# The relation layer of a graph network on one core: row fetching split into four pieces with the one-hot block stationary, and a new order of the work around it

## The chip, the cores and the metric

The kernel runs on one core of one Trainium2 chip. The metric is the device time of one execution in microseconds (us). A core has a matrix engine (TensorE, PE in the profile, with PEld for its weight loads), a vector engine (VectorE, DVE), a scalar engine (ScalarE, ACT), GpSimd (POOL) and a queue engine (SyncE, SP). The engines run their own instruction lists and wait for each other on semaphores. PE adds its products up in eight PSUM banks of 128 partitions by 512 fp32 values.

## The reference, cut to what matters

Two graph layers stand one behind the other. The first (two SAGE layers, a norm and a layer norm) is made with a dense adjacency and is not touched. The second, the relation layer, is what the change is about: 62,500 edges used of 6,250 nodes with 128 features, 32 relation types built from 8 basis matrices.

```python
hsrc = h[src]                       # rows of the edges' source nodes
coef = w_comp[etype]                # [edges, 8]
for b in range(8):
    msg = msg + hsrc @ weight[b] * coef[:, b][:, None]
msg = msg * norm
node_repr = jax.ops.segment_sum(msg, dst, num_segments=6250)
node_repr = jax.nn.relu(node_repr + bias)
x = layernorm(x + node_repr)
```

The edges are ordered by destination node.

## The kernel before

The first layer is built and run until about 2075 us of the profiled execution; from there to about 3830 us runs the relation layer. It works in STEPS = 114 steps. A step takes 10 tiles of 128 edges in order of destination (STEP_TILES), whose source rows GpSimd gathers from DRAM by an indirect DMA each (L797), and, in the first GROUPS = 112 steps, a group of PER = 4 further tiles of 128 edges that were sorted by their source node. The source nodes of a group lie in one of 7 classes of 7 blocks of 128 nodes (CLASS_BLOCKS), so their rows need no DMA: PE fetches them out of node rows that stay in SBUF, with a one-hot matrix. The node rows are kept as three bf16 parts whose sum is the fp32 value (XS part 0, XS part 1, and LOW).

What each engine does in step s:

* DVE makes `matrix` (L1719 to L1728: the place of an edge's node in a window times norm times the 8 coefficients), `wide_matrix` for the sorted group (L1735, L1736, L1741), the one-hot `ST2` of group s+2 (`sources`, L1749, 7 instructions of 512 columns), and adds PE's sums of every tile into rings of sums over nodes in SBUF (`tile_added`, L1769, 10 instructions, and `wide_added`, L1778, 4 instructions). Before the tile sums it reads the positions in the ring from a table (L1753 and the register loads with it, which the profile does not count as busy).
* PE makes `tiles_summed` (L1310: 5 fp32 products of 64 columns, twice per step), `sources` for the group of step s+2 (L1284: 21 bf16 products of 512 columns into bank 2, in the pieces 9, 6 and 6), `wide_summed` (L1327: 4 fp32 products of 336 columns), `coefficients` for step s+2 (L1266, L1270), `sources_turned` (L1319: 4 fp32 transposes of the fetched rows of group s+1), and in the 46 steps in which blocks of nodes are complete `block_multiplied` (L1346: 8 basis products for each of 51 blocks). 13 results are transposed at L1357.
* ACT makes `relations` (L972 to L981: the one-hot of edge types for step s+3), copies coefficients out of PSUM (L989), copies the fetched rows (L995) and the transposed rows (L1002), and takes a multiplied block with the bias (`block_taken`, L1021) and clears its place in the ring (L1026).
* SP issues the loads of edge types (L624, L629) and source rows (L637) and stores the results (L644).

Every engine works through its list in the order written. What comes out of PE goes through a ring of six PSUM banks (UNIT_BANKS); a unit (tile half, wide tile, turned group or result) waits in `unit_bank_free` until the unit six places before it has been added up by DVE, copied by ACT or taken. Blocks wait on DVE's additions (s_addg, s_adds) and on the coefficients copied (s_coefc); DVE's next additions into the ring wait for nothing else than their own bank except where ACT has cleared a block.

Of the kernel before, what the change touches and what calls it, by code (L numbers as in the profile page):

```python
# [91 lines left out]
SOURCE_PARTS = [(0, 3), (3, 5), (5, CLASS_BLOCKS)]  # L92
# [74 lines left out]
for step in range(STEPS):  # L167
    if step == 0:
        UNITS.append((0, "turn", 0))
# [4 lines left out]
    if step + 1 < GROUPS:  # L174
        UNITS.append((step + 1, "turn", 0))
# [60 lines left out]
def regular(nc, flag, x, src, dst, etype, w, w1, lin1, b1, lin2, b2, Wrel, wcomp, brel, out):  # L236
    with ExitStack() as ctx:
# [97 lines left out]
        GT = [unused[:, j * 512:(j + 1) * 512] for j in range(2)]  # L335
# [122 lines left out]
        s_turned = sem("sources_turned_copied")  # L458
# [342 lines left out]
        def _(act):  # L801
# [189 lines left out]
            def sources_copied(i):  # L991
                act.wait_ge(s_gs, i + 1)
                if i >= 2:
                    act.wait_ge(s_u, UNIT[i - 2, "turn", 0] + 1)
                nc.scalar.activation(GT[i % 2], bank(2), ACT.Copy).then_inc(s_gc, 1)  # L995

            def turned_copied(i):
                n = UNIT[i, "turn", 0]
                act.wait_ge(s_u, n + 1)
                if i >= 2:  # L1000
                    act.wait_ge(s_u, UNIT[i - 2, "wide", PER - 1] + 1)
                nc.scalar.activation(G2[i % 2].rearrange("p t c -> p (t c)"), bank(UNIT_BANKS[n % RING_BANKS]), ACT.Copy).then_inc(s_turned, 1)  # L1002
# [38 lines left out]
            turned_copied(0)  # L1041
            relations(2)
            sources_copied(1)
            for s in range(OUT_AT[-1] + 3):
                if KEPT_CHUNK + s < len(CHUNKS):
                    halved(KEPT_CHUNK + s)
                for n in events_in(s - 1):
                    block_taken(n)
# [5 lines left out]
                if s + 2 < STEPS:  # L1054
                    coefficients_copied(s + 2)
                if s + 1 < GROUPS:
                    turned_copied(s + 1)
                if s + 3 < STEPS:
                    relations(s + 3)

        @block.tensor
        def _(pe):
# [195 lines left out]
            def coefficients(s):  # L1258
# [3 lines left out]
                before = events_to(s - 3, lambda n: True)  # L1262
# [11 lines left out]
            def sources(i, part):  # L1274
                if part == 0:
# [3 lines left out]
                first = group_of(i) // ROUNDS_SORTED * CLASS_BLOCKS  # L1279
# [6 lines left out]
                if end == CLASS_BLOCKS:  # L1286
                    last.then_inc(s_gs, 1)

            def unit_bank_free(n):

                if n >= RING_BANKS:
# [5 lines left out]
                    elif kind == "turn":  # L1297
# [1737 lines left out]
```

## Time and profile before

| | us |
|---|---|
| median of three executions | 3764.12 |
| their range | 3760.8 to 3773.42 |
| the profiled execution: its span and own time | 3868.7 |
| first layer in it, about | 0 to 2075 |
| relation layer in it, about | 2075 to 3830 |

The profiled execution is 104.6 us (2.8%) longer than the median of the three, so times read from its trace are of a somewhat slower execution. In a row of a timeline stand the start, the duration, engine, line, operation, tiles and the count, and in brackets how long the engine was idle ahead of it and which instruction released it. "issue" means that nothing in the profile shows a wait; "remote" is a wait whose releaser the profile does not find. Ends of PE instructions are modelled, so the distance of two starts tells the pace better than a duration.

### The profile page before, as it was taken

What the parts mean: (1) busy time and instruction counts of PE and PEld (TensorE: products, weight loads), DVE (VectorE), ACT (ScalarE), POOL (GpSimd) and SP (SyncE); (2) the same over time, 40 slices, a digit from 0 to 9 for tenths busy, and PEclk for the clock granted to TensorE, in tenths of its full rate; (3) what the DMA queues carried; (4) which work ended last, traced back from release to release, by engine and by line L of the source; (5) the groups of instructions that cost most, each with busy time, mean ns of one, the idle gap of its engine ahead of it and who ended that gap; (6) DMA issues with size and microseconds to landing.
All of it is one profiled execution on the core that took longest, in us unless ns stands there. A gap on an engine that the chain in (4) does not pass through costs nothing.

```text
span 3868.7 us, 52705 instructions
## 1 busy us (share of the span) xinstructions
PE 3418.3 (88%) x17077; PEld 2281.2 (59%) x17077; DVE 2465.0 (64%) x4684; ACT 1351.6 (35%) x3452; POOL 2415.7 (62%) x2636
## 2 busy tenths in 40 slices
PE   3999999998999999999996888888988888988885
PEld 3899999984533344544443555556655556655554
DVE  7999999995776663022033666666656666666664
ACT  5999999990000000010002222222222222222221
POOL 5888888880036775555523666666666666666663
PEclk6999999999999999999998889888888888888897
DMA  6677777778779999999993222232222222222222
GB/s 185 192 206 205 206 208 208 208 205 291 263 233 256 269 259 269 301 271 275 293 298 93 65 66 70 60 78 70 70 57 71 65 74 67 73 65 69 67 66 46
DMA packets 532789, 618.45 MB, mean 160 GB/s; under 512 B 74011, under 2 KB 460127, under 8 KB 532399
## 3 DMA queue, kind: packets, MB, share of 16 engines
q1 hardware_dynamic: 478895, 528.52, 46.9%
q0 software_dynamic: 53616, 86.51, 8.9%
q8 instruction: 140, 2.29, 0.2%
q14 instruction: 138, 1.13, 0.1%
HBM read 445.83 MB, written 168.99 MB: 159 GB/s over the span
## 4 chain that ended last, share of the span: by engine, by line
PE 49%; ACT 19%; DVE 8%; issue 8%; DMA 7%; another core or an unknown queue 7%; DVEq 2%; POOL 1%; SPq 0%; ACTq 0%; POOLq 0%
PE PS L1231 21%; ACT arena L845 11%; PE PS L1284 10%; DMA arena<-adjacency 7%; ACT arena L861 6%; PE PS L1310 5%; PE PS L1327 5%; PE PS L1270 2%; PE PS L1119 2%; PE PS L1346 1%; DVE XT L1769 1%; PE PS L1319 1%; DVEq L1753 1%; DVE H L1749 1%
## 5 line engine op out<-in xcount | busy, mean ns | idle before, releaser
L797 POOL DMA_INDIRECT arena<-x_table,rec x1140 | 1159.6, 1017 | 613.0 <-issue 309.8
L776 POOL DMA_INDIRECT sorted_records<-arena x428 | 505.9, 1182 | 556.2 <-PE PS L1231 476.5
L1119 PE MATMUL PS<-arena 128*98 128x128 f32 x6272 | 761.6, 279 | 46.3 <-DVE arena L1508 13.0
L1119 PEld LDWEIGHTS PS<-arena 128*98 128x98 f32 x6272 | 708.4, 166 | 95.9 <-issue 50.4
L733 POOL TENSOR_SCALAR arena<-iota,H,arena 128x98 f32<-128x98 f32 x980 | 674.2, 702 | 91.7 <-PE PS L1119 89.2
L1284 PE MATMUL PS<-H,X 128*128 128x512 bf16 x1568 | 548.9, 436 | 74.5 <-issue 66.9
L845 ACT ACTIVATE arena<-arena 128x98 f32<-128x98 f32 x1568 | 582.9, 686 | 12.7 <-DVE arena L1506 12.6
L1231 PE MATMUL PS<-arena,X 128*128 128x512 f32 (+1 forms) x1274 | 541.4, 577 | 39.3 <-DMA arena<-adjacency 38.6
L1231 PE MATMUL PS<-arena,H 128*128 128x512 f32 (+1 forms) x1274 | 527.8, 570 | 16.0 <-DMA arena<-adjacency 15.5
L861 ACT ACTIVATE arena<-PS 98x1024 f32<-98x1024 f32 x392 | 519.6, 1325 | 12.5 <-PE PS L1119 12.5
L1769 DVE TENSOR_TENSOR XT<-XT,PS 128x64 f32 x1140 | 252.1, 221 | 421.6 <-issue 188.8
L1508 DVE TENSOR_TENSOR arena<-PS,H 128x2048 f32<-128x2048 f32 x196 | 447.0, 2280 | 0.0
L1687 DVE TENSOR_TENSOR arena<-arena 128x1536 f32<-128x1536 f32 (+1 forms) x192 | 343.9, 1791 | 157.2 <-DMA arena<-adjacency 151.5
L1231 PEld LDWEIGHTS PS<-arena,X 128*128 128x128 f32 x1274 | 237.4, 192 | 322.4 <-issue 193.3
L1231 PEld LDWEIGHTS PS<-arena,H 128*128 128x128 f32 x1274 | 238.5, 190 | 293.8 <-issue 215.3
L1310 PEld LDWEIGHTS PS<-arena 128*128 128x128 f32 x2280 | 320.6, 213 | 78.9 <-issue 46.8
L1310 PE MATMUL PS<-arena 128*128 128x64 f32 x2280 | 323.3, 292 | 46.5 <-issue 33.4
L1327 PE MATMUL PS<-arena 128*128 128x336 f32 x896 | 313.5, 472 | 43.5 <-issue 35.5
L1284 PE MATMUL PS<-H,arena 128*128 128x512 bf16 x784 | 337.6, 431 | 1.2 <-issue 1.0
L1778 DVE TENSOR_TENSOR arena<-arena,PS 128x336 f32 x448 | 224.7, 501 | 173.9 <-remote 75.7
L1284 PEld LDWEIGHTS PS<-H,X 128*128 128x128 bf16 x1568 | 172.5, 117 | 257.4 <-issue 162.9
L995 ACT ACTIVATE rec<-PS 128x512 f32<-128x512 f32 x112 | 66.7, 596 | 682.7 <-remote 439.7
(259 smaller groups left out, 3139.6 us busy)
## 6 DMA issues: line engine op xcount, KB each, us to landing
arena<-adjacency SPq DMA_DIRECT2D x294, 768.0 KB
adjacency<-arena SPq DMA_DIRECT2D x196, 784.0 KB
arena<-adjacency SPq DMA_DIRECT2D x98, 832.0 KB
arena<-x_table,rec POOLq DMA_INDIRECT x1140
XT<-sorted_source_rows SPq DMA_DIRECT2D x112, 128.0 KB
arena<-in_edge_type SPq DMA_DIRECT2D x226, 48.0 KB
arena<-in_edge_type SPq DMA_DIRECT2D x226, 32.0 KB
XT<-sorted_relations SPq DMA_DIRECT2D x448, 8.0 KB
```

The source lines that it names most:

```text
L733: last = nc.gpsimd.tensor_scalar(S1[:, r, :], iota[:, 0:M1], K1T[:, v:v + 1], WWT[:, v:v + 1], ALU.is_equal, ALU.mult)
L776: pool.indirect_dma_start(rec2_d, bass.IndirectOffsetOnAxis(ap=SLOT[:, t:t + 1], axis=0), R4[:, t, :], None).then_inc(s_scat, 16)
L797: pool.indirect_dma_start(G[:, n % HELD_UNITS * UNIT_TILES + i, :], None, x1_d, bass.IndirectOffsetOnAxis(ap=SRC[:, t:t + 1], axis=0)).the ...
L845: nc.scalar.activation(S1[:, r, :], S1[:, r, :], ACT.Copy, scale=WWT[:, v:v + 1]).then_inc(s_wa, 1)
L861: nc.scalar.activation(ST[0:M1, n % 3, q * GROUP * P:(q + 1) * GROUP * P], PS[0:M1, q * GROUP * P:(q + 1) * GROUP * P], ACT.Copy).then_inc ...
L1119: last = nc.tensor.matmul(bank(2 * q + j // 4, P, j % 4 * P)[0:M1, :], S1[:, r, :], S2[:, r, :], start=True, stop=True)
L1231: last = nc.tensor.matmul(bank(bank0 + c, nb * P), (X, H1)[l][:, k, :], AB[n % 4][:, off:off + nb * P], start=(k == 0), stop=(k == NBLK - 1))
L1284: last = nc.tensor.matmul(bank(2), rows_part, ST2[i % 2][:, j, :], start=(j == 0 and a == 0), stop=(j == CLASS_BLOCKS - 1 and a == 2))
L1310: last = nc.tensor.matmul(bank(UNIT_BANKS[n % RING_BANKS], BASIS, j * BASIS), G[:, half % HELD_UNITS * UNIT_TILES + j, :], C[s % 2][:, fir ...
L1327: nc.tensor.matmul(bank(UNIT_BANKS[n % RING_BANKS], WIDE_BASIS), G2[i % 2][:, c, :], C2[i % 2][:, c, :, :].rearrange("p b j -> p (b j)"), ...
L1508: nc.vector.tensor_tensor(S2[:, whole, :], bank(4, P).unsqueeze(1).to_broadcast([P, BATCH, P]), each(K2T, n).to_broadcast([P, BATCH, P]), ...
L1687: nc.vector.tensor_tensor(ACC[p % 2][:, 0:width], ACC[p % 2][:, 0:width], AB[n % 4][:, 0:width], ALU.add).then_inc(s_acc, 1)
```

## The change

`sources(i, c)` makes the fetched rows of one tile c of 128 edges at a time. The one-hot piece `ST2[:, j, c*128:(c+1)*128]` is the stationary side, the 128 columns of a part of the node rows are the moving side, and the result is [edge, feature], as `wide_summed` needs it. 84 products of 128 columns take the place of 21 of 512 columns. `sources_turned` on PE, `turned_copied` on ACT, the tile GT, the semaphore sources_turned_copied and the unit "turn" in the ring are gone. The four pieces stand in four places of PE's step. `coefficients(s+2)` moves ahead of the blocks; a block waits for the coefficients of step+4 rather than step+3. On ACT `relations(s+3)` and `coefficients_copied(s+2)` move from the end of a step to its start.

```diff
-SOURCE_PARTS = [(0, 3), (3, 5), (5, CLASS_BLOCKS)]
...
             def sources_copied(i):
                 act.wait_ge(s_gs, i + 1)
                 if i >= 2:
-                    act.wait_ge(s_u, UNIT[i - 2, "turn", 0] + 1)
-                nc.scalar.activation(GT[i % 2], bank(2), ACT.Copy).then_inc(s_gc, 1)
-
-            def turned_copied(i):
-                n = UNIT[i, "turn", 0]
-                act.wait_ge(s_u, n + 1)
-                if i >= 2:
                     act.wait_ge(s_u, UNIT[i - 2, "wide", PER - 1] + 1)
-                nc.scalar.activation(G2[i % 2].rearrange("p t c -> p (t c)"), bank(UNIT_BANKS[n % RING_BANKS]), ACT.Copy).then_inc(s_turned, 1)
+                nc.scalar.activation(G2[i % 2].rearrange("p t c -> p (t c)"), bank(2), ACT.Copy).then_inc(s_gc, 1)
...
             for s in range(OUT_AT[-1] + 3):
                 if KEPT_CHUNK + s < len(CHUNKS):
                     halved(KEPT_CHUNK + s)
+                if s + 3 < STEPS:
+                    relations(s + 3)
+                if s + 2 < STEPS:
+                    coefficients_copied(s + 2)
                 for n in events_in(s - 1):
                     block_taken(n)
...
                 if s + 2 < GROUPS:
                     sources_copied(s + 2)
-                if s + 2 < STEPS:
-                    coefficients_copied(s + 2)
-                if s + 1 < GROUPS:
-                    turned_copied(s + 1)
-                if s + 3 < STEPS:
-                    relations(s + 3)
...
-                before = events_to(s - 3, lambda n: True)
+                before = events_to(s - 4, lambda n: True)
...
-            def sources(i, part):
-                if part == 0:
+            def sources(i, c):
+                first = group_of(i) // ROUNDS_SORTED * CLASS_BLOCKS
+                if c == 0:
                     pe.wait_ge(s_st2, i + 1)
                     if i:
                         pe.wait_ge(s_gc, i)
-                begin, end = SOURCE_PARTS[part]
-                pe.wait_ge(s_low, CHUNK_OF[first + end - 1] + 1)
-                for j in range(begin, end):
+                for j in range(CLASS_BLOCKS):
+                    if c == 0 and i < CLASSES:
+                        pe.wait_ge(s_low, CHUNK_OF[first + j] + 1)
                     for a, rows_part in enumerate((XS[:, first + j, 0, :], XS[:, first + j, 1, :], LOW[:, first + j, :])):
-                        last = nc.tensor.matmul(bank(2), rows_part, ST2[i % 2][:, j, :],
+                        last = nc.tensor.matmul(bank(2, D, c * D), ST2[i % 2][:, j, c * P:(c + 1) * P], rows_part,
                                                 start=(j == 0 and a == 0), stop=(j == CLASS_BLOCKS - 1 and a == 2))
...
-                pe.wait_ge(s_turned, i + 1)
+                pe.wait_ge(s_gc, i + 1)
...
-                pe.wait_ge(s_coefc, min(step + 3, STEPS))
+                pe.wait_ge(s_coefc, min(step + 4, STEPS))
...
             for s in range(OUT_AT[-1] + 1):
+                ahead = s + 2 < GROUPS
                 if s < STEPS:
                     tiles_summed(s, 0)
-                if s + 2 < GROUPS:
+                if ahead:
                     sources(s + 2, 0)
                 if s < GROUPS:
                     wide_summed(s, 0)
                     wide_summed(s, 1)
-                if s + 2 < GROUPS:
+                if ahead:
                     sources(s + 2, 1)
+                if s + 2 < STEPS:
+                    coefficients(s + 2)
                 for n in events_in(s - 1):
                     block_multiplied(n)
                 if s < GROUPS:
                     wide_summed(s, 2)
                     wide_summed(s, 3)
+                if ahead:
+                    sources(s + 2, 2)
                 if s < STEPS:
                     tiles_summed(s, 1)
-                if s + 2 < GROUPS:
-                    sources(s + 2, 2)
-                if s + 2 < STEPS:
-                    coefficients(s + 2)
-                if s + 1 < GROUPS:
-                    sources_turned(s + 1)
+                if ahead:
+                    sources(s + 2, 3)
```

PE's list before, from the end of the second row-fetching piece of a step in which a block is multiplied, to its first transposes (H is part of the kept one-hots and rows, wcd the relation coefficients, Wr the basis matrices):

```order
L1284 MATMUL PS<-H,arena 128x512
L1346 MATMUL PS<-XT,Wr 128x128 [waits messages_rectified,coefficients_copied,gathered_sums_added]
L1346 MATMUL PS<-XT,Wr 128x128 x7
L1327 MATMUL PS<-arena 128x336 [waits wide_matrix_made,sources_turned_copied,sorted_sums_added]
L1327 MATMUL PS<-arena 128x336 [waits wide_matrix_made,sources_turned_copied,gathered_sums_added]
L1310 MATMUL PS<-arena 128x64 [waits nodes_gathered3,matrix_made,sources_turned_copied]
...
L1266 MATMUL PS<-wcd,XT 128x32 [waits messages_rectified,coefficients_copied,relations_marked]
L1270 MATMUL PS<-wcd,arena 128x32 x2
L1270 MATMUL PS<-wcd,arena 128x16
L1319 MATMUL PS<-ident,rec 128x128 [waits sources_copied,gathered_sums_added]
```

PE's list after the change at the same block, from the end of the second piece:

```order
L1267 MATMUL PS<-X,H 128x128 x2
L1267 MATMUL PS<-arena,H 128x128
L1249 MATMUL PS<-wcd,XT 128x32 [waits messages_rectified,coefficients_copied,relations_marked]
L1253 MATMUL PS<-wcd,arena 128x32 x2
L1253 MATMUL PS<-wcd,arena 128x16
L1319 MATMUL PS<-XT,Wr 128x128 [waits messages_rectified,coefficients_copied,gathered_sums_added]
L1319 MATMUL PS<-XT,Wr 128x128 x7
L1300 MATMUL PS<-arena 128x336 [waits wide_matrix_made,sources_copied,sorted_sums_added] x2
```

The coefficients' products now stand directly ahead of the block, whose wait on coefficients_copied is for these same coefficients, and the wide tiles behind the block wait on sources_copied alone.

ACT's list before, of the same step, from the block it takes to the last instruction of `relations`:

```order
L1021 ACTIVATE H<-PS,bcol 128x128 [waits basis_sums_made,blocks_multiplied]
L1026 ACTIVATE XT<-zero 128x8x128
L995 ACTIVATE rec<-PS 128x512 [waits basis_sums_made,sources_multiplied]
L989 ACTIVATE XT<-PS 128x112 [waits wide_matrix_made,matrix_made,coefficients_multiplied]
L1002 ACTIVATE arena<-PS 128x512 [waits basis_sums_made]
L972 ACTIVATE H<-arena,rel_of 128x256 [waits types_spread1,coefficients_multiplied]
L973 ACTIVATE H<-arena,rel_of 64x128
L976 ACTIVATE XT<-XT,rel_of 128x128 [waits sorted_types_spread1]
L978 ACTIVATE H<-H,ones 128x256 [waits relations_apart]
L979 ACTIVATE H<-H,ones 64x128
L981 ACTIVATE XT<-XT,ones 128x128
```

ACT's list after the change, of the same step:

```order
L965 ACTIVATE H<-arena,rel_of 128x256 [waits types_spread1,coefficients_multiplied]
L966 ACTIVATE H<-arena,rel_of 64x128
L969 ACTIVATE XT<-XT,rel_of 128x128 [waits sorted_types_spread1]
L971 ACTIVATE H<-H,ones 128x256 [waits relations_apart]
L972 ACTIVATE H<-H,ones 64x128
L974 ACTIVATE XT<-XT,ones 128x128
L982 ACTIVATE XT<-PS 128x112 [waits wide_matrix_made,matrix_made,coefficients_multiplied]
L1007 ACTIVATE H<-PS,bcol 128x128 [waits basis_sums_made,blocks_multiplied]
L1012 ACTIVATE XT<-zero 128x8x128
L988 ACTIVATE arena<-PS 128x512 [waits basis_sums_made,sources_multiplied]
```

`relations`, with its waits on the loaded edge types, and the copy of the coefficients now stand ahead of the block and its clearing. The lists of DVE, GpSimd and SyncE are the same before and after.

## Rows read from the trace of the kernel before

**Rows 1.** The page: busy time of each engine.

```profile
PE 3418.3 (88%) x17077; PEld 2281.2 (59%) x17077; DVE 2465.0 (64%) x4684; ACT 1351.6 (35%) x3452; POOL 2415.7 (62%) x2636
```

**Rows 2.** Windows, 2165 to 3830 us: length, busy PE, PEld, DVE, ACT, POOL, clock.

```profile
2165.00:3830.00 1665.00, 1425.71 (x7330) 974.64 (x7330) 1063.34 (x3167) 430.34 (x1066) 1100.37 (x1084) 0.87 0.27 68
```

**Rows 3.** Timeline of PE, one step at full clock.

```profile
3027.17 1.23 PE L1310 MATMUL PS<-arena 128*128 128x64 f32 x10
3028.23 0.59 PE L1284 MATMUL PS<-H,X 128*128 128x512 bf16 x2
...
3033.73 1.22 PE L1310 MATMUL PS<-arena 128*128 128x64 f32 x10
3034.79 0.59 PE L1284 MATMUL PS<-H,X 128*128 128x512 bf16 x2
...
3036.09 0.30 PE L1266 MATMUL PS<-wcd,XT 128*128 128x32 f32 x2
...
3037.09 0.66 PE L1319 MATMUL PS<-ident,rec 128*128 128x128 f32 x4
3037.58 0.56 PE L1310 MATMUL PS<-arena 128*128 128x64 f32 x2
```

**Rows 4.** Timeline of DVE, one step without long waits.

```profile
3354.44 1.63 DVE L1769 TENSOR_TENSOR XT<-XT,PS 128x64 f32 x5 [2.79 <-issue]
...
3362.65 0.50 DVE L1778 TENSOR_TENSOR arena<-arena,PS 128x336 f32 x1
...
3367.63 0.93 DVE L1769 TENSOR_TENSOR XT<-XT,PS 128x64 f32 x3 [2.22 <-issue]
```

**Rows 5.** Groups by line, 2165 to 3830 us: count, busy, mean ns, idle before.

```profile
L797 POOL DMA_INDIRECT arena<-x_table,rec x1084 | 1101.8, 1016 | 564.4 <-issue 294.2 <-PE PS L1310 124.9 <-remote 118.0
```

**Rows 6.** Waits of DVE, 2165 to 3830 us: total, times, longest.

```profile
DVE arena L1778 <- remote: 75.7, 29, 6.7
...
DVE XT L1769 <- remote: 45.1, 14, 4.9
...
DVE arena L1778 <- ACT arena L1026: 18.1, 7, 4.9
DVE arena L1778 <- PE PS L1310: 11.1, 10, 4.7
DVE arena L1778 <- PE PS L1327: 9.1, 7, 4.7
DVE arena L1778 <- ACT XT L1026: 6.9, 5, 2.0
```

**Rows 7.** Timeline of PE, early: pairs of a load and a 1-column product.

```profile
1002.84 1.96 PE L1184 MATMUL PS<-ones_h,H 128*128 128x1 bf16 x28
```

**Rows 8.** Timeline of PE at half clock.

```profile
2959.42 1.06 PE L1284 MATMUL PS<-H,X 128*128 128x512 bf16 x2
2960.28 0.63 PE L1284 MATMUL PS<-H,arena 128*128 128x512 bf16 x1
```

**Rows 9.** Groups of the whole span: the transposes.

```profile
L1319 PE MATMUL PS<-ident,rec 128*128 128x128 f32 x448 | 84.7, 316 | 6.8 <-issue 6.8
```

**Rows 10.** Timeline of SyncE behind a stored result.

```profile
2789.63 0.41 SPq L644 DMA_DIRECT2D out<-H  x1
...
2792.55 1.84 SPq L629 DMA_DIRECT2D arena<-in_edge_type  x4
```

**Rows 11.** Timeline of ACT there: `relations`, first and last instruction.

```profile
2787.94 0.50 ACT L972 ACTIVATE H<-arena,rel_of 128x256 f32<-128x256 int32 x1
...
2789.76 0.38 ACT L981 ACTIVATE XT<-XT,ones 128x128 f32<-128x128 f32 x1
```

**Rows 12.** Timelines of PE and ACT: a block multiplied, a ring place cleared.

```profile
2965.67 1.95 PE L1346 MATMUL PS<-XT,Wr 128*128 128x128 f32 x16
...
2972.79 1.04 ACT L1026 ACTIVATE XT<-zero 128x1024 f32<-128x1024 f32 x1
```

**Rows 13.** Timeline of DVE there: the third wide tile.

```profile
2803.94 0.50 DVE L1778 TENSOR_TENSOR arena<-arena,PS 128x336 f32 x1
```

More of the change, by code:

```diff
@@ L167 @@
 for step in range(STEPS):
-    if step == 0:
-        UNITS.append((0, "turn", 0))
     UNITS.append((step, "tile", 0))
@@ L173 @@
     UNITS.append((step, "tile", 1))
-    if step + 1 < GROUPS:
-        UNITS.append((step + 1, "turn", 0))
     UNITS += [(step, "result", m) for m in range(len(OUT_AT)) if OUT_AT[m] == step]
@@ L334, in regular @@
         ST2 = [h1_flat[:, j * HALF_ST2:(j + 1) * HALF_ST2].bitcast(BF16).rearrange("p (k e) -> p k e", e=PER * P) for j in range(2)]
-        GT = [unused[:, j * 512:(j + 1) * 512] for j in range(2)]
         G2 = [cut(17280 + j * PER * D, PER * D).rearrange("p (t c) -> p t c", c=D) for j in range(2)]
@@ L457, in regular @@
         s_u = sem("basis_sums_made")
-        s_turned = sem("sources_turned_copied")
         s_bp = sem("blocks_multiplied")
@@ L1040, in _ @@
             sources_copied(0)
-            turned_copied(0)
             relations(2)
@@ L1278, in sources @@
                         pe.wait_ge(s_gc, i)
-                first = group_of(i) // ROUNDS_SORTED * CLASS_BLOCKS
-                begin, end = SOURCE_PARTS[part]
-                pe.wait_ge(s_low, CHUNK_OF[first + end - 1] + 1)
-                for j in range(begin, end):
+                for j in range(CLASS_BLOCKS):
+                    if c == 0 and i < CLASSES:
+                        pe.wait_ge(s_low, CHUNK_OF[first + j] + 1)
                     for a, rows_part in enumerate((XS[:, first + j, 0, :], XS[:, first + j, 1, :], LOW[:, first + j, :])):
-                        last = nc.tensor.matmul(bank(2), rows_part, ST2[i % 2][:, j, :],
+                        last = nc.tensor.matmul(bank(2, D, c * D), ST2[i % 2][:, j, c * P:(c + 1) * P], rows_part,
                                                 start=(j == 0 and a == 0), stop=(j == CLASS_BLOCKS - 1 and a == 2))
-                if end == CLASS_BLOCKS:
+                if c == PER - 1:
                     last.then_inc(s_gs, 1)
@@ L1296, in unit_bank_free @@
                         pe.wait_ge(s_adds, added_wide(step, i))
-                    elif kind == "turn":
-                        pe.wait_ge(s_turned, step + 1)
                     else:
@@ L1312, in tiles_summed @@
                 last.then_inc(s_u, 1)
-            def sources_turned(i):
-                n = UNIT[i, "turn", 0]
-                unit_bank_free(n)
-                pe.wait_ge(s_gc, i + 1)
-                for c in range(PER):
-                    last = nc.tensor.transpose(bank(UNIT_BANKS[n % RING_BANKS], P, c * P), GT[i % 2][:, c * P:(c + 1) * P], ident[:])
-                last.then_inc(s_u, 1)
             def wide_summed(i, c):
@@ L1364, in _ @@
             for i in range(2):
-                for part in range(len(SOURCE_PARTS)):
-                    sources(i, part)
-                if i == 0:
-                    sources_turned(0)
+                for c in range(PER):
+                    sources(i, c)
             pe.wait_ge(s_zero, 2)
             for s in range(OUT_AT[-1] + 1):
+                ahead = s + 2 < GROUPS
                 if s < STEPS:
                     tiles_summed(s, 0)
-                if s + 2 < GROUPS:
+                if ahead:
                     sources(s + 2, 0)
```

## The prediction

> **What bounds the kernel now.** I read the busy shares first. PE is busy 88% of the span, DVE 64% [rows 1], and in the relation layer PE has 1425.7 of 1665 us [rows 2]. That looks like a PE bound, and a change that adds 63 products to each step would then be paid in full. A share doesn't tell why an engine is busy, though: PE's clock is 0.87 in this window [rows 2], so part of its work ran at half speed, and a PE that is late only because it has time does no harm. So I read single steps next. At full clock a PE step runs from 3027.17 to 3037.58, 10.41 us, from its first tile products to those of the next step [rows 3]. A DVE step without long waits runs from 3354.44 to 3367.63, 13.19 us, from one step's first ring addition to the next's, with table reads in it that the profile shows as "issue" [rows 4]. GpSimd's gathers take (1101.8 + 294.2) / 1084 = 1.29 us each, "issue" included, 12.9 us for ten [rows 5]. DVE, with GpSimd close behind it, is the longest of the three by 2.8 us over PE.
>
> Does that account for the layer? The window holds 109 steps (1084 gathers of ten a step, and a few), 15.3 us each. 109 steps of 13.19 us are 1438 us. Waits of DVE without a known releaser add 75.7 + 45.1 = 120.8 us in 43 cases, and waits with PE or ACT as releaser 18.1 + 11.1 + 9.1 + 6.9 = 45.2 us in 29 cases [rows 6]. That makes 1604 of 1665 us; about ten results of some 5 us on DVE (an estimate: they are in no row here) fill most of the rest. So at most some 45 us of the layer is visibly owed to a late PE or ACT. The 120.8 us are close to the 104.6 us by which the profiled execution is longer than the median, and I take them to be its own: the sum below is made on the median of 3764, and the same differences would hold on the 3868.7 us of the profiled execution.
>
> **The change part by part.**
>
> *Row fetching.* Now 21 products of 512 columns; six of them stand between 3034.79 and 3036.09, 0.217 us each [rows 3], 4.55 us a step. Then 84 products of 128 columns, each with a weight load of its own. No row shows that pair, so I bound it. From below: a quarter of 0.217, 0.054 us, if the load hides wholly behind the product ahead of it. From above: 28 pairs of a bf16 load and a product of only one column took 1.96 us, 0.070 us each [rows 7], which is the pace of loads alone; if load and product hid nothing of each other it would be 0.070 + 0.054 = 0.124. The profile calls PEld overlapping with PE and 974.6 us of loads lie beside 1425.7 us of products in 1665 us [rows 2], so they overlap; the time is then the larger of the two, 0.054 to 0.070. I take 0.060, as some of the 28 ends are pipeline latency: 84 × 0.060 = 5.04 us, +0.5 us a step. At half clock two products of 512 columns took 2960.28 − 2959.42 = 0.86 us, 0.43 each [rows 8], so a quarter is 0.107: 84 of them take 9.0 us, as 21 took, and the load is hidden sooner.
>
> The Trainium skill speaks against the change here: "TensorE: Matmul & The Clock Gate", section "Back-to-back issue gap", gives a sustained stream of load and product pairs of 128 columns about 81 ns each, against 56 ns for an isolated gap. By that estimate the pieces would take 6.8 us. The trace has no stream of such pairs; its nearest row gives 0.070.
>
> *Transposes.* 448 are gone: four took 3037.58 − 3037.09 = 0.49 us [rows 3], 84.7 us busy and 6.8 us idle over the span [rows 9]. Together with the pieces PE's step is 10.41 + 0.50 − 0.49 = 10.4 us, unchanged, still 2.8 us under DVE's: no cost and no gain. ACT's copy of 0.6 us a step goes too; ACT is busy 430 of 1665 us [rows 2], so it is worth nothing by itself.
>
> *Way of a late PE to the next wide tile.* Where PE is late behind a block, its catching up counts. Before, from the wide tiles behind a block to those of the next step: tiles 1.06 (3033.73 to 3034.79), row fetching 1.30, coefficients 1.00 (3036.09 to 3037.09), transposes 0.49, tiles 1.06, row fetching 9 × 0.217 = 1.95; 6.86 us [rows 3]. After: 3 × 21 × 0.060 + 2 × 1.06 = 5.90. That is 0.96 us less. The 29 waits [rows 6] are the places where it can count: at most 29 × 0.96 = 28 us, at least nothing. About half of them (12, on ACT's clearing of a block) end at a block in the same step, which the shorter way does not bring forward, and at the others a part is swallowed by waits behind them: I take half, −14 us.
>
> *Coefficients ahead of the block.* In 46 steps the block now stands behind 1.00 us of coefficient products and a wait for ACT's copy of them, some 0.65 us (an estimate: PE's drain, and a copy of a fifth of the 512-column copy). The third wide tile comes 1.65 us later in PE's step. DVE asks for it 3362.65 − 3354.44 = 8.21 us after its step's first addition [rows 4], in which it does its matrices and the one-hot, so I cost it at nothing; without that cover it would be 46 × 1.65 = 76 us at most.
>
> *ACT's new order.* `relations` waits for edge types from SyncE; behind it now stand the coefficients' copy, the block, its clearing and the copy of fetched rows, and behind these PE's block and DVE. SyncE is late where a result is stored: the store stood at 2789.63 and the last type load began at 2792.55 + 1.84 = 2794.39 [rows 10]. With some 2 us to land (0 to 5.5 as bounds; no row shows one of these landings), `relations` of 2.2 us (2787.94 to 2790.14 [rows 11]), 0.3 us for the copy, 1.95 us for a block [rows 12], an estimated 0.4 us for taking it and 1.04 us for clearing [rows 12], that is 2802.3; DVE took the third wide tile at 2803.94 [rows 13]. The margin is 1.6 us, −1.8 at the late bound and 3.7 at the early one. Six steps are of this kind (a stored result and a block in one step); with a late bound and a second block of 2 to 3 us the loss is 6 × 4.7 = 28 us; I take 8.
>
> Sum: 3764 + 0 − 14 + 8 = 3758 us.
>
> **The rivals.**
>
> *PE is the real bound (gain).* For it: 88% busy and 1425.7 of 1665 us [rows 1, 2]. Then the 91.5 us of transposes [rows 9] come back less what the pieces cost, 112 × 0.5 = 56, so −35 at 0.060 and −72 at 0.056: between 3729 and 3692, say 3710. Against it: only 45.2 us of DVE's waits name PE or ACT. Chance 0.20.
>
> *Nothing moves.* Late steps come from DVE's and GpSimd's own work, the credit and the loss are both taken up by the waits that follow: 3764 ± 5. Chance 0.12.
>
> *ACT's order costs (slower).* The place is `relations` at the head of a step with a stored result; from a landing later than 3.6 us behind the issue it decides. Price 28 us, and no credit: 3792. For it: SyncE's issues alone take 4.8 us there [rows 10]. Against it: the margin worked out above. Chance 0.15.
>
> *The loads don't hide (slower).* The point from which it decides is the pace at which PE's mean step reaches DVE's 13.19. PE's is 10.41 − 0.49 − 4.55 = 5.37, and blocks add 51 × 1.95 / 112 = 0.89, the wait ahead of them 0.27; so 6.53 + 84 × t reaches 13.19 at t = 0.079. At 0.124 PE's step is 16.9 us against a mean of (1665 − 120.8) / 109 = 14.2: +2.7 × 112 = +302, 4066 us. Just above 0.079, with a half clock here and there, 10 to 40 us: about 3790. Chance 0.13, nearly all of it for the small price. The page named above puts the pace, 81 ns, at this very point.
>
> **How the numbers follow.** The forecast has the rest, 0.40, with a range of its own of 3738 to 3772. Of the time of this kernel 0.3% is 11.3 us, about what its measurement can tell from no change: 3753 to 3775. The forecast of 3758 lies just inside; of its 0.40 I give 0.17 to faster, 0.22 to the same, 0.01 to slower. Faster: 0.17 + 0.20 = 0.37. The same: 0.22 + 0.12 + 0.02 of the slower rivals = 0.36. Slower: 0.01 + 0.26 = 0.27. The range reaches into the gain (3700) and takes in both small prices (3800); beyond stand the end of the gain and a pace far over 0.079, under 2 in 10 together.
>
> **What the profile of the changed kernel would show.** The pace of the 128-column products, from starts: 0.054 to 0.070 proves the first step, 0.08 and more the last rival. DVE's steps without waits stay at 13.2 us, and its waits on PE and ACT fall from 45 us to about 31 if the credit is right; they rise at the wide tiles, with ACT's clearing or PE's block as releaser, in the six steps with a stored result if ACT's order costs, and `relations` is then seen to wait for a DMA. PE's step at full clock stays near 10.4 us, with a gap of about 0.65 us ahead of a block. PE's clock may change with the 84 short products in place of the long ones; the median would show it only if PE became the last to end. The prediction is wrong if DVE's step is not what paces the layer, or if waits that I gave to the profiled execution are in every execution and follow from PE's list of instructions, which grows by half.

## The result, and the profile after

On the chip on which the kernel before took 3764.03 us (median of six), the changed kernel took 3785.76 us (median of six, 3779.66 to 3789.87). The medians are 21.7 us apart; the ratio with its 95% interval, 1.0048 (1.0033 to 1.0063), makes it 18 us (12 to 24). The forecast was 3758 us, by a small gain.

A second result came with the experiments. On three other chips the same two programs took 3880 and 4759, 3894 and 4755, and 3868 and 4738 us: ratios 1.2244, 1.2225 and 1.2256. On a fourth the kernel before took 3744 us. So there are two kinds of chip for this kernel; I call them first kind (3744 to 3764 us before) and second kind (3868 to 3911 us before). One chip of the second kind came twice, with 3894 and 3911 us, and no chip was seen to change its kind. The profile of before [rows 1 to 13] with its 3868.7 us looks like the second kind, and its median came from the first. Not only its time says so. PE's waits ahead of row fetching without a releaser, 2165 to 3830 us, in before and then in before_again, which ran on a second-kind chip:

```profile
PE PS L1284 <- issue: 55.6, 26, 7.0
PE PS L1284 <- issue: 73.8, 39, 8.2
```

No profile of a first-kind chip, or of a kernel with direct loads (below), has more than 1.5 us of them.

The page and the windows of the changed kernel, profiled on the chip of the 3786 us (columns as in [rows 2]):

```profile
PE 3328.4 (88%) x23685; PEld 2497.3 (66%) x23685; DVE 2467.1 (65%) x4684; ACT 1294.2 (34%) x3340; POOL 2413.3 (64%) x2636
...
2165.00:3750.00 1585.00, 1353.74 (x13915) 1203.96 (x13914) 1090.68 (x3238) 381.43 (x973) 1149.80 (x1111) 0.92 0.30 73
```

6608 more products, and PE is still 88% busy. The clock is 0.92 in place of 0.87, but on a chip of the other kind; before_plain below, without the change, has 0.92 too. PE's waits, and those of DVE, in 2165 to 3740 us (total, times, longest):

```profile
PE PS L1267 <- DVE H L1721: 86.1, 55, 2.5
PE PS L1319 <- issue: 56.9, 35, 8.6
PE PS L1300 <- DVE arena L1713: 49.0, 61, 1.9
```

```profile
DVE XT L1741 <- PE PS L1300: 116.5, 45, 3.2
...
DVE XT L1741 <- PE PS L1291: 13.1, 8, 2.8
DVE arena L1750 <- ACT XT L1012: 4.7, 3, 2.4
DVE arena L1750 <- PE PS L1300: 4.3, 11, 1.0
...
DVE arena L1750 <- ACT arena L1012: 3.5, 1, 3.5
DVE arena L1750 <- PE PS L1291: 2.9, 10, 0.6
```

PE waits for DVE's one-hot and for the wide matrix, which is how a PE looks that has time. The 116.5 us in the first row of DVE stand ahead of the tile sums, where DVE reads its table: 2.6 us each, where the same place without a releaser takes 2.4 (151.6 us in 64 cases), so hardly more than that reading. The "remote" waits, 120.8 us in [rows 6], are gone: they belong to the other kind of chip, for before_again has 63.1 and 43.0 us of them in the same window. New are PE's waits of up to 8.6 us ahead of a block (L1319), and on ACT the wait of `relations` for edge types, which stands at 131 us in the groups by line:

```profile
L965 ACT ACTIVATE H<-arena,rel_of 128x256 f32<-128x256 int32 x55 | 27.5, 500 | 40.6 <-DMA arena<-in_edge_type 40.6
...
L965 ACT ACTIVATE arena<-arena,rel_of 128x256 f32<-128x256 int32 x54 | 27.0, 501 | 90.5 <-DMA arena<-in_edge_type 90.5
```

Most of it costs nothing, since ACT is ahead. Where it costs, one sees in a step with a stored result and a block. The timelines of SyncE, ACT, PE and DVE in step 52:

```profile
2878.09 0.41 SPq L637 DMA_DIRECT2D out<-H  x1
...
2881.00 1.86 SPq L622 DMA_DIRECT2D arena<-in_edge_type  x4
```

```profile
2885.37 0.51 ACT L965 ACTIVATE H<-arena,rel_of 128x256 f32<-128x256 int32 x1 [13.24 <-DMA arena<-in_edge_type]
...
2887.49 0.24 ACT L982 ACTIVATE XT<-PS 128x112 f32<-128x112 f32 x1
2891.44 0.37 ACT L1007 ACTIVATE H<-PS,bcol 128x128 f32<-128x128 f32 x1 [3.71 <-PE PS L1319]
2891.70 1.05 ACT L1012 ACTIVATE XT<-zero 128x1024 f32<-128x1024 f32 x1
```

```profile
2887.83 3.57 PE L1319 MATMUL PS<-XT,Wr 128*128 128x128 f32 x16 [7.80 <-issue]
2891.24 1.30 PE L1300 MATMUL PS<-arena 128*128 128x336 f32 x4
```

```profile
2883.34 1.64 DVE L1741 TENSOR_TENSOR XT<-XT,PS 128x64 f32 x5 [2.21 <-issue]
...
2892.89 0.50 DVE L1750 TENSOR_TENSOR arena<-arena,PS 128x336 f32 x1 [1.39 <-ACT XT L1012]
...
2894.96 1.64 DVE L1741 TENSOR_TENSOR XT<-XT,PS 128x64 f32 x5 [0.85 <-PE PS L1291]
```

The loads are issued until 2882.86, `relations` starts at 2885.37, 2.5 us later, the coefficients are copied at 2887.73, and only then may PE start its block, though these coefficients were multiplied 8 us before and the block's sums were ready as well. The block then takes 3.57 us where it took 1.95 [rows 12]: after 7.8 us without work PE runs its first products at half clock. The windows of the changed kernel around it (columns as in [rows 2], the clock third from the end):

```profile
2884.00:2887.80 3.80, 0.00 (x0) 0.00 (x0) 3.20 (x11) 2.33 (x7) 0.69 (x1) 0.53 0.52 116
2887.80:2891.20 3.40, 3.37 (x16) 3.40 (x17) 3.33 (x9) 0.00 (x0) 0.00 (x0) 0.52 0.11 31
2891.20:2893.00 1.80, 1.80 (x18) 1.34 (x18) 0.41 (x2) 1.31 (x2) 0.00 (x0) 1.00 0.25 62
```

The granted clock is at the lower of the two levels, 1.2 GHz, for nearly all of the block, and at 2.4 GHz behind it. DVE's third wide tile waits 1.39 us for ACT's clearing, and 0.85 us more are lost at the next tile sums. The step takes 16.1 us. The 1.6 us by which the block is longer are more than either of these waits: at full clock this step would have lost next to nothing (an estimate from these rows, not run).

### The profile page after: what moved, and what is told of

It reads as the page before. It is cut to its first block, busy times and chain, and to the rows that moved or that the text cites. A ratio compares the mean times of both kernels' runs of the same rounds, so it can differ in the third digit from the quotient of the medians.

```text
span 3785.2 us, 65588 instructions
## 1 busy us (share of the span) xinstructions
PE 3328.4 (88%) x23685; PEld 2497.3 (66%) x23685; DVE 2467.1 (65%) x4684; ACT 1294.2 (34%) x3340; POOL 2413.3 (64%) x2636
## 4 chain that ended last, share of the span: by engine, by line
PE 35%; DVE 21%; ACT 18%; DMA 10%; issue 9%; DVEq 6%; POOL 1%; SPq 0%; POOLq 0%
PE PS L1214 20%; ACT arena L838 11%; DMA arena<-adjacency 10%; ACT arena L854 6%; DVE H L1721 5%; DVE XT L1741 5%; DVEq L1725 5%; PE PS L1267 4%; PE PS L1300 3%; DVE arena L1750 2%; PE PS L1319 2%; PE PS L1291 2%; PE PS L1102 2%; DVE arena L1700 1%; DVEq L1741 1%
## 5 line engine op out<-in xcount | busy, mean ns | idle before, releaser
L790 POOL DMA_INDIRECT arena<-x_table,rec x1140 | 1179.4, 1035 | 463.8 <-issue 325.2
L769 POOL DMA_INDIRECT sorted_records<-arena x428 | 483.8, 1130 | 626.3 <-PE PS L1214 548.3
L1267 PE MATMUL PS<-X,H 128*128 128x128 bf16 x6272 | 610.5, 227 | 89.2 <-DVE H L1721 86.1
L1267 PEld LDWEIGHTS PS<-X,H 128*128 128x128 bf16 x6272 | 521.6, 103 | 163.2 <-DVE H L1721 96.0
L1267 PE MATMUL PS<-arena,H 128*128 128x128 bf16 x3136 | 583.2, 227 | 0.0
L1300 PE MATMUL PS<-arena 128*128 128x336 f32 x896 | 337.7, 503 | 49.1 <-DVE arena L1713 49.0
L1291 PE MATMUL PS<-arena 128*128 128x64 f32 x2280 | 299.2, 280 | 27.3 <-DVE H L1778 19.8
L1267 PEld LDWEIGHTS PS<-arena,H 128*128 128x128 bf16 x3136 | 319.6, 102 | 0.0
L1291 PEld LDWEIGHTS PS<-arena 128*128 128x128 f32 x2280 | 280.5, 196 | 30.6 <-DVE H L1778 21.4
L1478 DVE TENSOR_TENSOR arena<-PS,H 128x1078 f32<-128x1078 f32 x196 | 250.6, 1278 | 41.2 <-PE PS L1102 34.1
```

The source lines that it names most:

```text
L769: pool.indirect_dma_start(rec2_d, bass.IndirectOffsetOnAxis(ap=SLOT[:, t:t + 1], axis=0), R4[:, t, :], None).then_inc(s_scat, 16)
L790: pool.indirect_dma_start(G[:, n % HELD_UNITS * UNIT_TILES + i, :], None, x1_d, bass.IndirectOffsetOnAxis(ap=SRC[:, t:t + 1], axis=0)).the ...
L1267: last = nc.tensor.matmul(bank(2, D, c * D), ST2[i % 2][:, j, c * P:(c + 1) * P], rows_part, start=(j == 0 and a == 0), stop=(j == CLASS_B ...
L1291: last = nc.tensor.matmul(bank(UNIT_BANKS[n % RING_BANKS], BASIS, j * BASIS), G[:, half % HELD_UNITS * UNIT_TILES + j, :], C[s % 2][:, fir ...
L1300: nc.tensor.matmul(bank(UNIT_BANKS[n % RING_BANKS], WIDE_BASIS), G2[i % 2][:, c, :], C2[i % 2][:, c, :, :].rearrange("p b j -> p (b j)"), ...
```

## The experiments

All kernels of one group ran on one chip; "beside" stands the median of the kernel before on that chip, and the ratio behind a time is to it. The loads on GpSimd were replaced in some of them (names with _plain), which turned a chip of the second kind into one that behaves like the first:

```diff
-pool.indirect_dma_start(G[:, n % HELD_UNITS * UNIT_TILES + i, :], None, x1_d, bass.IndirectOffsetOnAxis(ap=SRC[:, t:t + 1], axis=0))
+pool.dma_start(G[:, n % HELD_UNITS * UNIT_TILES + i, :], x1_d[t % 48 * P:(t % 48 + 1) * P, :])
```

**The same two programs again, and each half of the change.** pieces_only is the changed kernel with this undone:

```diff
 # ACT                                   # PE
-relations(s + 3) at the step's head     -coefficients(s + 2) ahead of the blocks
+relations(s + 3) at its end             +coefficients(s + 2) behind sources(s + 2, 3)
-coefficients_copied(s + 2) at the head  -wait_ge(s_coefc, min(step + 4, STEPS)), events_to(s - 4)
+coefficients_copied(s + 2) at the end   +wait_ge(s_coefc, min(step + 3, STEPS)), events_to(s - 3)
```

order_only is the kernel before with just these lines the other way round.

> The kernel before, unchanged, for a second profile. In the first profiled execution the last adjacency product of the first layer ended at 2053.0 us and DVE's ring additions ran from 2110.7 us; after the change they stood at 2100.4 and 2145.3 us. Theory A (the two relation layers differ little or the new one is faster; the first layer, whose code is the same, runs slower in the changed program): here the first layer ends near 2053 again and the loop from DVE's first ring addition to its last takes 1610 to 1640 us without the 105 us of waits that were in the first profile. Theory B (the first layer's end varies from execution to execution by 50 us, and the relation layer is the slower part): the first layer ends anywhere between 2050 and 2100, and the loop takes about 1590 us. Time 3764 by both.

> The changed kernel, unchanged, for a second profile. Theory A: the first layer ends near 2100 us again, the loop takes 1611 us. Theory B: the first layer ends elsewhere by tens of us. Time 3786 by both.

> The changed kernel with ACT's order, the place of the coefficients' products and the block's waits as before: only the row fetching is turned round, in four pieces. Theory A (first layer slower in a program with more instructions): near 3786, first layer ends near 2100. Theory C (the new order of relations and coefficients costs in the relation layer, by waits on loaded edge types, 131 us of ACT in the profile after): 3764 or less. Theory D (the 84 short products cost): 3780 to 3790 with the first layer ending near 2053.

> The kernel before with only the new order: on ACT relations and the copy of coefficients at the head of a step, on PE the coefficients' products ahead of the blocks, the block's wait for step+4 and the coefficients' for events to s-4; row fetching in three pieces of 512 columns and its transposes stay. Theory A: the first layer ends near 2053 and the time is 3764 or some us less, as the number of PE instructions stays. Theory C: 3775 to 3790. Theory D: 3764.

Measured, on a second-kind chip, beside 3879.67 us: before_again 3894.41 (1.0027), after_again 4759.03 (1.2244), pieces_only 4132.99 (1.0628), order_only 4101.59 (1.0549). None of the theories had this. The first layer's last adjacency product, which stood at 2053 us in the profile before and at 2100 us in that after, ended at 2070, 2072, 2084 and 2078 us here: it moves by tens of us between profiles, and on one chip it is the same for both programs (2070 and 2072 us), so theory A falls. On this chip all the rest lies in the relation layer, and the split of the change was masked by a far larger effect.

What that effect is, the timelines of PE and GpSimd in after_again show:

```profile
3025.94 0.28 PE L1267 MATMUL PS<-X,H 128*128 128x128 bf16 x2
3026.05 0.22 PE L1267 MATMUL PS<-arena,H 128*128 128x128 bf16 x1
3026.99 0.27 PE L1267 MATMUL PS<-X,H 128*128 128x128 bf16 x2 [0.72 <-issue]
3028.44 0.22 PE L1267 MATMUL PS<-arena,H 128*128 128x128 bf16 x1 [1.17 <-issue]
3029.86 0.22 PE L1267 MATMUL PS<-X,H 128*128 128x128 bf16 x1 [1.21 <-issue]
3031.98 0.26 PE L1267 MATMUL PS<-X,H 128*128 128x128 bf16 x1 [1.90 <-issue]
...
3035.48 0.40 PE L1267 MATMUL PS<-X,H 128*128 128x128 bf16 x2 [0.30 <-issue]
```

```profile
3021.34 0.94 POOL L790 DMA_INDIRECT arena<-x_table,rec  x1 [10.54 <-PE PS L1291]
...
3032.56 0.94 POOL L790 DMA_INDIRECT arena<-x_table,rec  x1 [0.30 <-issue]
```

Products that wait for nothing in the profile start 0.7, 1.4 or 2.1 us apart in place of 0.06. This begins 5 us behind the first of ten gathers and ends some 2 us behind the last (3021.3 to 3033.5 here; PE is slow from 3026.3 to 3035). It is so in 104 of the 107 runs of ten gathers in the window, with 4.9 to 6.0 us for the begin and 1.7 to 2.0 us for the end; in 27 runs a single product is late before that, 2 us behind the first gather. PE's waits and DVE's there, 2165 to 4700 us:

```profile
PE PS L1267 <- issue: 678.4, 825, 1.9
...
DVE arena L1750 <- remote: 662.1, 107, 7.6
```

**Direct loads in place of the gathers.**

> The kernel before, unchanged, on whichever chip this group runs. The two chips so far gave two pictures: on the one the pair took 3764 and 3786 us, on the other 3880 and 4759. If this is a chip of the first kind, its profile shows where the 21 us lie: theory F (in the first layer or its end, whose code is the same, so that the relation layer is even): first layer ends near 2079, the loop takes about 1610. Theory G (in the relation layer): first layer ends near 2100 as in the profile after, the loop takes about 1590. On a chip of the second kind: 3880, first layer ends near 2070, loop 1735.

> The changed kernel, unchanged, on the same chip as the kernel before. First kind of chip: 3786, loop 1611 us. Second kind: 4759, with PE's short products issued at 0.7 us a pair from about 5 us behind the start of a run of ten gathers to 2 us behind its end.

> The kernel before with each of GpSimd's 1140 indirect gathers replaced by a direct load of 128 rows that lie together (so the rows fetched are not those of the edges). Theory H (GpSimd's gathers, 1.25 us each and one a step of 2.1 us beside DVE's widest instruction, pace the loop at 13.55 us a step): 30 to 60 us faster than the kernel before, then DVE at 13.2 us. Theory K (DVE alone paces it): no faster. On a chip of the second kind, if the gathers are what slows PE's issue: back to about 3730.

> The changed kernel with the same direct loads in place of the indirect gathers (the rows fetched are not those of the edges). First kind of chip: the same 30 to 60 us below the changed kernel. Second kind: if the indirect gathers are what slows PE's issue of short products, the 0.7 us steps are gone and the time falls by some 900 us to about that of the kernel before with the same loads; if they have nothing to do with it, it stays at 4700.

Another second-kind chip, beside 3894.24 us: before_third 3888.92 (0.9998), after_third 4755.08 (1.2225), before_plain 3717.85 (3716.41 to 3724.53), after_plain 3733.74 (3730.90 to 3740.62). The indirect gathers are what slows PE on this kind: without them the changed kernel is 1021 us faster, the one before 176 us. And the pair that is left differs by 15.9 us, 0.43%, nearly the ratio of the result. That lies in the relation layer (loop 1566.6 and 1587.6 us), as theory G had it for the first kind. Here the two profiles can be laid beside each other, step by step. Lines of these kernels that lie behind the edit stand one lower than in the originals.

**Which half costs the 0.4%.** relations_last is the changed kernel with one move on ACT:

```diff
 for s in range(OUT_AT[-1] + 3):
-    if s + 3 < STEPS:
-        relations(s + 3)
     if s + 2 < STEPS:
         coefficients_copied(s + 2)
...
         sources_copied(s + 2)
+    if s + 3 < STEPS:
+        relations(s + 3)
```

> The kernel before with only the new order (ACT's relations and copy of coefficients at the head of a step, PE's coefficients ahead of the blocks) and with direct loads of 128 rows that lie together in place of the indirect gathers, so that the rows fetched are not those of the edges. With such loads the kernel before took 3717.9 and the changed kernel 3733.7 us. Theory L (relations at the head waits for edge types that SyncE issues late behind a stored result, and holds up block and ring): 3732 to 3740, the loss in steps 27, 52, 65, 78, 81 and 91. Theory D (the 84 short products cost it): 3718.

> Only the row fetching in four pieces, the order of relations and coefficients as before, with the same direct loads. Theory L: 3716 to 3720. Theory D: 3730 to 3736.

> The changed kernel with ACT's relations back at the end of a step; the copy of coefficients stays at the head, PE's order stays as changed; the same direct loads. Theory L: 3716 to 3722, with steps 27, 52, 65, 78, 81, 91 as in the kernel before. If it is the wait of the block for the coefficients of step+4 that costs, not relations: 3733 still.

> The same with the indirect gathers of the kernel, that computes the reference. On a chip where the pair takes 3764 and 3786: 3764 +/- 8 by theory L. On a chip where it takes 3885 and 4757 PE's issue during the gathers decides: pieces alone took 4133 and order alone 4102 there, and I expect between 4133 and 4757, below the changed kernel.

This group ran on a first-kind chip, beside 3743.79 us. order_plain took 3723.89, pieces_plain 3720.18, relations_last_plain 3713.06 us; relations_last, with the real gathers, 3748.93 us, ratio 1.0004 (0.9992 to 1.0016). relations_last_plain came out below its range (3716 to 3722), order_plain below that of theory L (3732 to 3740). Moving `relations` back to the end of ACT's step brings the changed kernel from 1.0048 to 1.0004, on two chips of the first kind; the two were not run side by side on one such chip. The lengths of DVE's steps (first ring addition to the next step's first, us), worked out from the starts in the traces, say where (loop is from the first step's start to the last one's):

```
step   before_  pieces_  order_   relations_  after_   relations_  after
       plain    plain    plain    last_plain  plain    last
27     13.1     13.1     13.6     13.1        15.0     13.3        15.3
52     13.6     13.7     14.5     13.6        17.0     13.9        16.1
65     13.4     13.4     13.6     13.5        14.1     13.6        16.2
78     13.7     13.7     14.6     13.6        15.0     13.6        18.3
81     13.1     13.1     13.0     13.1        15.0     13.3        15.1
91     13.1     13.1     15.7     13.1        20.1     13.1        17.5
loop   1566.6   1567.5   1572.8   1570.3      1587.6   1596.4      1610.7
```

before_plain and after_plain ran on the second-kind chip of 3894 us, after on the chip of the result, the other four on the chip of 3744 us. With direct loads chips can be compared by steps: before_plain and pieces_plain, on two kinds of chip, agree to 0.1 us in all six.

These six steps, the ones with a stored result and a block, add up to 80.0 us in before_plain and 96.2 in after_plain: 16.2 of the loop's 21.0 us. The changed kernel has 98.5 in them, relations_last 80.8, though the whole loop of relations_last is only 14.3 us shorter: its step 56 alone takes 18.9 us against 14.0, for a reason not looked into. In step 91 of after_plain, ACT and PE:

```profile
3400.59 0.51 ACT L964 ACTIVATE arena<-arena,rel_of 128x256 f32<-128x256 int32 x1 [8.95 <-DMA arena<-in_edge_type]
...
3402.71 0.24 ACT L981 ACTIVATE XT<-PS 128x112 f32<-128x112 f32 x1
```

```profile
3403.05 3.75 PE L1318 MATMUL PS<-XT,Wr 128*128 128x128 f32 x16 [6.44 <-issue]
3407.35 3.75 PE L1318 MATMUL PS<-arena,Wr 128*128 128x128 f32 x16 [0.55 <-ACT H L1006]
```

In the same step of before_plain:

```profile
3384.54 2.05 PE L1345 MATMUL PS<-XT,Wr 128*128 128x128 f32 x16
3387.14 2.02 PE L1345 MATMUL PS<-arena,Wr 128*128 128x128 f32 x16 [0.55 <-ACT H L1020]
```

The first block starts 2.8 us ahead of DVE's step (3387.3 us) there, and 4.3 us behind its start (3398.7 us) in after_plain, with both blocks at half clock.

The pieces by themselves cost nothing: loop +0.9 us. Order by itself costs 6.2 us in the loop, less than the 14 to 22 expected; with pieces and order together `relations` gets its types later in DVE's step (1.8 us behind its start in step 91, against 0.5 us in order_plain). The stored result stands at the same place in both, 5.84 us ahead of the step. Behind it one issue of a load on SyncE is longer in after_plain: 1.45 us in place of 0.50 in step 91, and by 0.6 and 1.1 us in steps 52 and 81. Why these issues are longer is not shown.

**Second kind of chip, real gathers.**

> The changed kernel beside the three below. On a chip of the first kind, where the kernel before takes 3740 to 3765: 1.005 of it, the loop 14 to 21 us longer than with relations last, in steps 27, 52, 65, 78, 81 and 91. On a chip of the second kind: 4757.

> The kernel before with the new order alone. First kind of chip: 1.001 to 1.003 of the kernel before (6 us were measured in the loop with direct loads, 21 for order and pieces together). Second kind: 4102.

> Row fetching in four pieces alone. First kind of chip: 0.999 to 1.001. Second kind: 4133.

> The changed kernel with relations at the end of ACT's step. First kind of chip: 0.999 to 1.001, so 0.995 of the changed kernel. Second kind: if the order of relations brings the slow issue, near 4133 as with the pieces alone; if it is the place of the coefficients and the even spacing of PE's short products, near 4757.

Beside 3868.05 us: after_fourth 4737.97 (1.2256), order_second 4067.22 (1.0536), pieces_second 4108.60 (1.0631), relations_last_second 4737.16 (1.2257). With the pieces in, the 870 us of this kind do not hang on the place of `relations`. The pieces bring 6%, the order 5%, both 23%; what is left of the order beside the pieces is the early place of the coefficients on PE and of their copy. Whether `relations` matters without the pieces was not run. In order_only the cost stands ahead of the blocks: PE waits 216.1 us in 36 cases there (2165 to 3830 us), against 3.3 us in 2 cases in before.

**A third of PE's row fetching.** Two of the three row parts are left out, in the changed kernel with relations last and in the kernel before:

```diff
-for a, rows_part in enumerate((XS[:, first + j, 0, :], XS[:, first + j, 1, :], LOW[:, first + j, :])):
+for a, rows_part in enumerate((XS[:, first + j, 0, :],)):
```

> The changed kernel with relations last, row fetching from the first of the three row parts alone (two parts are left out, so the fetched rows have bf16 precision): 28 products of 128 columns a step in place of 84. Theory M (number of instructions that PE issues during the gathers decides on the second kind of chip): 3850 to 4100 there, against 4737. If the number is of no matter: above 4600. On the first kind of chip DVE and GpSimd pace the loop: no faster than 0.998 of the kernel before.

> The kernel before, row fetching from the first row part alone (two parts left out): 7 products of 512 columns a step in place of 21. Theory M, second kind of chip: 14 of some 75 products of a step go, so a third or more of the 130 us by which such a chip is slower than the first kind; 3800 to 3850. First kind of chip: 0.996 to 1.0 of the kernel before, as DVE and GpSimd pace it.

Second kind again, beside 3910.91 us: 4144.46 (1.0584) and 3880.51 (0.9919). With 56 products fewer a step the new orientation is about 600 us faster than relations_last (4737 on another chip of this kind), so the number of instructions that PE has to issue during the gathers matters; but both missed the range of theory M. The 5.8% that are left are not the price of the 28 short products alone, for this kernel has the early coefficients too, and order_only, with as many products as the kernel before (17077), costs 5.5% on such a chip. For the same reason the number alone is not the whole law: where the products stand counts as well. The 28 products without the new order were not run.

## Why the prediction was wrong

*DVE paces the loop at 13.2 us, PE has time*: right in that PE does not pace it, with GpSimd nearer than I had it. In the changed kernel undisturbed steps take 13.2 and 14.0 us in turn, so the one step that I read was one of the shorter ones. With direct loads they take 13.05 and 13.65. The 45.2 us of DVE's waits on PE and ACT leave out two rows of the same view, which stand at the tile sums:

```profile
DVE XT L1769 <- PE PS L1327: 57.0, 20, 5.4
```

The other has 6.2 us on L1310. Most of both is the reading of the table, 2.3 us each time, which the 13.19 us hold already; some 11 us are waiting. The 45.1 us of "remote" waits on the same line hold that reading too.

*Pace of the short products*: right, 0.054 to 0.070 stated, 0.060 taken. In the timeline of PE after:

```profile
2133.95 0.22 PE L1267 MATMUL PS<-arena,H 128*128 128x128 bf16 x1
2134.00 0.28 PE L1267 MATMUL PS<-X,H 128*128 128x128 bf16 x2
2134.11 0.22 PE L1267 MATMUL PS<-arena,H 128*128 128x128 bf16 x1
```

Two in 0.11 us, some 0.056 each, in a stream of pairs with a load each. The 81 ns of the Trainium skill ("TensorE: Matmul & The Clock Gate", section "Back-to-back issue gap") do not hold in this stream; the 56 ns that it gives for an isolated gap do. (In the rival on PE as the real bound the gain at 0.056 comes to 74 us, not 72.) A full-clock step, from the tile sums at 3146.40 to those at 3156.95 us, takes 10.55 us, for 10.4 forecast.

*The credit of −14 us* for the shorter way of a late PE was wrong. relations_last_plain has this shorter way, and its loop is 3.7 us longer than that of before_plain; pieces_plain, whose coefficients stand behind the block again, has the old length of way and +0.9 us. DVE's waits on PE and ACT in [rows 6] were read from a chip of the other kind. Without the late gathers there is next to nothing to win: in before_plain the wide tiles wait 2.8 us for PE's tile sums (L1309) and 1.5 us for its transposes (L1318) in the whole layer.

*Coefficients ahead of the block, at nothing*: right on the first kind of chip, since relations_last keeps them there and stands at 1.0004.

*ACT's new order at 8 us* is the step that failed, in its size. The place, the six steps, the chain and its rival (3792 us) were right, and the rival should have been the forecast: measured +17.7 us in these steps, changed kernel against relations_last, and +16.2 with direct loads. The margin of 1.6 us was the error. From the last load's issue to the end of the clearing I had 7.9 us, and 9.55 until DVE takes its third wide tile. In step 52 the chain takes 10.0 us (2882.86 to 2892.89) and DVE is ready after 8.6, so the margin is −1.4. Of these 3.0 us, 1.6 are the block, which runs at half clock behind the 7.8 us in which PE waited for the coefficients; 0.5 are the landing, 2.5 us in place of 2; and 0.9 are the loads, which stand that much nearer to DVE's step (issued until 0.5 us ahead of it). I had read the 9.55 in step 45 of a second-kind profile, which has a stored result but no block. The other five steps look the same: first blocks of 3.65 to 3.75 us behind 6.4 to 8.7 us without work, and landings of 2.2 to 3.4 us.

With 0 for 14 and the measured 17.7 for 8 the sum is 3782 us; 3785.8 were measured, and the ratio with its interval says 3776 to 3788. Without the failed term the forecast would still have had the wrong sign, by the credit. That ACT's order is worth some 0.44% is shown by relations_last, on another chip of the same kind; that it is worth the same on the very chip of the result was not run.

*The waits given to the profiled execution*: I took 120.8 us of waits without releaser for a matter of one execution. They are a matter of the chip: before_again has 106.1 us of them. And they are what the new row fetching multiplies on such a chip (662.1 us on one line in after_again).

## What to carry to other kernels

An instruction that waits on a DMA belongs behind those that the critical engines wait for, even if it stands ready nearly always: six late loads cost all that the change had to lose. When PE is left idle by such a wait, price what follows at half clock: here a block took 3.6 to 3.75 us behind 5.0 to 8.7 us without work, and 1.95 to 2.05 us at full clock. And if the profile and the times disagree by more than their spread, treat them as two machines, and do not carry a wait from the one into a sum for the other.

## What the runs showed of the hardware

The pace at which PE issues independent bf16 products can fall from 0.06 us to multiples of 0.7 us while GpSimd issues indirect gathers: on three of the four chips of the experiments and not on the chip of the result, and not with direct loads of the same 64 KB on one of the three. The changed kernel was 22% slower than the one before there and 0.5% on the chip of the result. What it is in these chips was not settled. Longer transfers of instructions it is not, as far as the packets of their queue tell; after_again in 2165 to 4700 us, and the changed kernel on the first kind in 2165 to 3740 us (packets, MB, share of 16 engines):

```profile
q8 instruction: 112, 1.84, 0.3%
q8 instruction: 112, 1.84, 0.5%
```

Both come to about 1.1 us a packet. The long products of the kernel before suffer far less (3 to 4% between the kinds, 3744 or 3764 against 3868 to 3911 us).

A gather of 0.94 us took 1.5 to 2.3 us beside one DVE instruction, the wide matrix, in 91 of 112 steps of the changed kernel on the first kind, and never over 1.4 us elsewhere. Timelines of GpSimd and DVE in the changed kernel, first kind:

```profile
3132.59 0.94 POOL L790 DMA_INDIRECT arena<-x_table,rec  x1 [0.31 <-issue]
3133.84 2.10 POOL L790 DMA_INDIRECT arena<-x_table,rec  x1 [0.30 <-issue]
```

```profile
3133.56 1.56 DVE L1713 TENSOR_TENSOR arena<-XT 128x1344 f32<-128x1344 f32 x1
```

Ten gathers with the one shown make 9 × 1.25 + 2.4 = 13.6 us, the mean of 13.2 and 14.0. So on the first kind of chip GpSimd's gathers pace the undisturbed steps together with DVE, and direct loads bring 36 us there (relations_last 3748.93, relations_last_plain 3713.06 us, on one chip).
